# The v tile asked for behind the store and the x tile: SyncE's order of requests in the mixing stage of a two-layer kernel on one Trainium2 core

## The chip, the cores and the metric

The kernel runs on one core of one Trainium2 chip. The metric is the device time of one execution in microseconds (us), as the median over several runs. Lower is better. The core has five engines with a queue of instructions each: PE (TensorE, matmuls), DVE (VectorE), ACT (ScalarE), POOL (GpSimd) and SP (SyncE, which computes nothing and here only waits and issues DMA transfers). DMA transfers that SP issues appear in the profile as hardware queue q1, those that POOL issues as software queue q0.

## What is computed

The input x is (2, 48, 512, 512) in float32. Layer 0 adds to x a channel attention over 4x4 blocks, and layer 1 adds to that four directional scans. Cut to what the change touches:

```
# layer 0, on the normalized x
qkv = depthwise3x3(conv1x1(x))               # q, k, v, in 8 heads
q, k, v -> (b, heads, 6 * 4 * 4 = 96, 128 * 128)
attn = softmax(q_hat @ k_hat.T * temperature)     # 96 x 96 for each head
out = attn @ v                               # MIXING: this stage
out = proj 1x1 (48 channels) of out, put back in rows and columns
x1 = x + out                                 # MIXING: the sum with x
# layer 1: x1 + four scans (down, up, right, left) of the normalized x1
```

## The kernel before, in words

The program has five stages, one after the other: statistics of x, a first pass over x that makes q, k and v and writes v to DRAM (`v_blocks`), the mixing, the four scans, and a final sum. The change touches the mixing stage alone, in `attention_weights_and_mix`.

Mixing first computes the 96x96 attention weights (`attT`). Then it goes over 64 groups: 2 batches (`B`) of 32 groups (`G`), and a group is 16 image rows of 48 channels (`T` = 16). A group is 4 tiles of 4 rows (`NB` = 4). For group j the engines do this:

- PE: for each of the 4 tiles, 8 matmuls per head set with the v tile (`a_ps<-attT,v_in`, L812; the function `group`), whose end counts up the semaphore `att_done`; 8 transposes (`t_ps<-eye,mixed`, L800; `turn`); and two projections (`o_ps<-turned,projd`, L790; `project`). The projections in group j are those of group j - 1: PE works one group behind itself there.
- ACT copies between PSUM and SBUF for PE (L848, L853).
- DVE: four times per group it adds the projected rows in PSUM to the rows of x (`scan_t<-o_ps,res`, L931, four instructions), which counts up the semaphore `summed`, and takes statistics (`bn_stats`, L942, two instructions). It does this for group j - 1 while PE mixes group j.
- SP: three transfers for each group: the next v tile (`load_v`, L698, 1536 KB on 96 partitions, into one of two slots of `v_in`), the store of the lower half of the finished sum (`store`, L691, `x_scan<-scan_t`, 768 KB on 48 partitions), and the lower half of the x tile (`load_res`, L685, `res<-x`, 768 KB on 48 partitions).
- POOL: two transfers for each group, the upper halves of that store and of that x tile (`upper_half`, the same two lines).

What orders SP's requests is the order in which they are written, and two waits. A v slot is free when PE has mixed the group that used it, so the load of v(j + 1) waits for `att_done` of 4j (all tiles of group j - 1 mixed). The store of group j - 2 waits until `summed` shows that group as added up; the x tile of group j then goes into the slot that those sums have left. SP waits in order: what stands behind a waiting instruction is not issued. The waits of the engines that use the data are these: PE waits at the start of group j + 1 for its v tile (`v_landed`), and DVE waits before its first sum of group j for both halves of the x tile and for the stores that free the slot of `scan_t` (`res_landed`, `scan_out`).

The rounds of the loop `Fori(1, G // 2 - 1)` do this for most groups, and `turnover` for the four groups at a batch's two ends. The first three v tiles are asked for ahead of all this and do not move.

Of the kernel before, what the change touches and what calls it, by code (L numbers as in the profile page):

```python
# [638 lines left out]
def attention_weights_and_mix(nc, sem, sumsq, ones, gram_sb, temp, eye, x, projT, attT, v_blocks, x1_scan, x1_stats, x1_mv):  # L639
# [5 lines left out]
    with ExitStack() as ctx:  # L645
# [35 lines left out]
        def batch_of(j):  # L681
            return divmod(j, G)

        def load_res(queue, b, g, s, half):
            queue.dma_start(res[ODD * half:ODD * half + C, s],  # L685
                            x[b, :, bass.ds(T * g + NP * half, NP)]).then_inc(res_landed[half][s], 16)

        def store(queue, b, g, s, q):

            queue.wait_ge(summed, N * G * b + N * g + N)  # L690
            queue.dma_start(x1_scan[b, :, bass.ds(g, 1), q].rearrange("c g t w -> c (g t) w"),  # L691
                            scan_t[ODD * q:ODD * q + C, s]).then_inc(scan_out[q][s], 16)

        with nc.Block() as block:
            @block.sync
            def _(sp):
                def load_v(b, g, s):
                    sp.dma_start(v_in[:, s].rearrange("p h i n -> p h (i n)"),  # L698
                                 v_blocks[b, bass.ds(g, 1)].rearrange("g p h n -> (g p) h n")).then_inc(v_landed[s], 16)

                def next_v(j):

                    sp.wait_ge(att_done, NB * j)
                    load_v(*batch_of(j + 1), (j + 1) % 2)

                def turnover(j):

                    if j + 1 < GROUPS:
                        next_v(j)
                    store(sp, *batch_of(j - 2), j % 2, 0)  # L710
                    load_res(sp, *batch_of(j), j % 2, 0)

                sp.dma_start(temp_sb[:], temp.broadcast_to([HD, HEADS])).then_inc(params, 16)
                for s in range(2):
                    load_v(0, s, s)
                sp.wait_ge(proj_clear, 1)
                for q in range(2):
                    sp.dma_start(projd[ODD * q:ODD * q + C, ODD * q:ODD * q + C], projT).then_inc(proj_in, 16)
                for s in range(2):
                    load_res(sp, 0, s, s, 0)  # L720
                next_v(1)
                for b in range(B):
                    if b:
                        turnover(b * G)
                        turnover(b * G + 1)
                    with sp.Fori(1, G // 2 - 1) as i:
                        for s in range(2):

                            sp.wait_ge(att_done, NB * G * b + NB * (2 * i + s))
                            load_v(b, 2 * i + s + 1, 1 - s)  # L730
                            store(sp, b, 2 * i + s - 2, s, 0)
                            load_res(sp, b, 2 * i + s, s, 0)
                    turnover(b * G + G - 2)
                    turnover(b * G + G - 1)
                for s in range(2):
                    store(sp, B - 1, G - 2 + s, s, 0)
                for s in range(2):
                    sp.wait_ge(scan_out[0][s], 16 * (GROUPS // 2))
# [783 lines left out]
```

## Time and profile before

| what | value |
|---|---|
| median of 3 runs | 10613.97 us (10603.93 to 10615.23) |
| the profiled execution, its own time | 10620.18 us |
| its span, first to last instruction | 10618.6 us |
| PE busy over the span | 9390.0 us (88%) |
| DVE busy over the span | 8088.3 us (76%) |
| DMA traffic | 2101.31 MB, mean 198 GB/s |

The rows further down come from the profiled execution, so a sum worked out from them is made against its 10620.18 us, and that is 6.2 us above the median. PE's busy time is modelled at its ends, so a busy PE is not a PE at its peak; idle gaps on PE are real waits.

### The profile page before, as it was taken

The numbers are of one execution on the slowest core, as the hardware profiler recorded it, in microseconds if no ns is written. First come the engines' busy times: TensorE is split into PE (matmuls) and PEld (weight loads), VectorE is DVE, ScalarE is ACT, GpSimd is POOL, SyncE is SP. The second block draws the span as 40 slices with busy tenths as digits, with TensorE's granted clock in tenths as the row PEclk, the third lists the DMA queues.
The fourth block names the chain that finished last, engine by engine and source line by source line (L and its number), as shares of the span: only waits on it lengthen the run. The fifth ranks groups of instructions, "written<-read, shape, count | busy, mean of one in ns | idle before, by whom it ended". The sixth has DMA issues, their size and how long they took to land. (4 is left out here: it accounts for less than half of the span.)

```text
span 10618.6 us, 213374 instructions
## 1 busy us (share of the span) xinstructions
PE 9390.0 (88%) x72742; PEld 9046.5 (85%) x72742; DVE 8088.3 (76%) x16184; ACT 6343.3 (60%) x11046; POOL 2941.8 (28%) x4237
## 2 busy tenths in 40 slices
PE   0799999999999998999979999999999999999200
PEld 0699999999999998777769999999999999999200
DVE  7777777777777776888877777777799997777333
ACT  0577777767777776443446667999933336666100
POOL 0000000000000000000026666666666666666100
PEclk9999999999999999999989999999999999999655
DMA  9566666666666666899978897777766666777899
GB/s 365 121 131 132 132 131 129 132 118 133 133 132 130 132 133 118 238 256 247 261 174 202 201 202 183 210 214 214 211 208 217 214 212 171 205 199 198 338 431 406
DMA packets 726580, 2101.31 MB, mean 198 GB/s; under 512 B 56944, under 2 KB 631568, under 8 KB 635360
## 3 DMA queue, kind: packets, MB, share of 16 engines
q1 hardware_dynamic: 611920, 1794.63, 65.9%
q10 hardware_dynamic: 106368, 204.76, 6.2%
q0 software_dynamic: 8192, 100.67, 3.4%
q8 instruction: 51, 0.84, 0.0%
q14 instruction: 49, 0.40, 0.0%
HBM read 1344.64 MB, written 754.97 MB: 198 GB/s over the span
## 5 line engine op out<-in xcount | busy, mean ns | idle before, releaser
L1363 ACT CAST hi<-rough 112x256 fp32r<-112x256 f32 x4096 | 1666.9, 407 | 1402.5 <-DVE rough L1277 1352.7
L1197 PE MATMUL scan_ps<-hi,scan_high 112*112 112x256 f32 x12264 | 2123.3, 281 | 32.3 <-ACT hi L1363 32.3
L1277 DVE SCALAR_TENSOR_TENSOR rough<-scan_ps,scan_bias,lines 112x256 f32<-112x256 f32 x4086 | 2136.7, 523 | 18.7 <-issue 15.0
L1208 PE MATMUL scan_ps_low<-lo,scan_high 112*112 112x256 f32 x12264 | 2126.3, 282 | 0.5 <-POOL lo L1309 0.5
L1203 PE MATMUL scan_ps_low<-hi,scan_low 112*112 112x256 f32 x12264 | 2121.4, 281 | 0.0
L488 PE MATMUL conv_ps<-tap_high,x_high 128*128 128x432 f32 (+2 forms) x6144 | 1879.3, 306 | 45.1 <-DVE x_edge L568 31.7
L488 PE MATMUL conv_ps<-tap_low,x_high 128*128 128x432 f32 (+2 forms) x6144 | 1906.6, 310 | 0.0
L488 PE MATMUL conv_ps<-tap_high,x_low 128*128 128x432 f32 (+2 forms) x6144 | 1906.4, 310 | 0.0
L1197 PEld LDWEIGHTS scan_ps<-hi,scan_high 112*112 112x112 f32 x12264 | 1691.2, 176 | 33.7 <-ACT hi L1363 33.1
L1208 PEld LDWEIGHTS scan_ps_low<-lo,scan_high 112*112 112x112 f32 x12264 | 1686.3, 175 | 3.4 <-POOL lo L1309 0.9
L1203 PEld LDWEIGHTS scan_ps_low<-hi,scan_low 112*112 112x112 f32 x12264 | 1684.0, 176 | 0.0
L1309 POOL TENSOR_TENSOR lo<-lines,hi 112x256 fp32r<-112x256 f32 x2048 | 1418.5, 693 | 802.7 <-DVE lines L1282 779.4
L1309 POOL TENSOR_TENSOR lo<-ring,hi 112x256 fp32r<-112x256 f32 x2048 | 1419.8, 693 | 769.1 <-DVE ring L1282 763.8
L368 ACT ACTIVATE x_high<-raw,negmean 128x512 fp32r<-128x512 f32 x1024 | 1217.2, 1247 | 62.5 <-DMA raw_edge<-x 51.5
L564 DVE SCALAR_TENSOR_TENSOR x_low<-raw,negmean,x_high 128x512 fp32r<-128x512 f32 x1024 | 1150.3, 1153 | 118.9 <-ACT x_high L368 118.9
L1282 DVE TENSOR_TENSOR ring<-scan_ps_low,rough 112x256 f32<-112x256 f32 x2044 | 869.0, 425 | 467.9 <-PE scan_ps_low L1208 432.3
L488 PEld LDWEIGHTS conv_ps<-tap_high,x_high 128*128 128x128 f32 x6144 | 1161.5, 189 | 66.6 <-DVE x_edge L568 33.3
L488 PEld LDWEIGHTS conv_ps<-tap_low,x_high 128*128 128x128 f32 x6144 | 1162.5, 189 | 20.8 <-issue 0.2
L488 PEld LDWEIGHTS conv_ps<-tap_high,x_low 128*128 128x128 f32 x6144 | 1165.0, 190 | 17.3
L1282 DVE TENSOR_TENSOR lines<-scan_ps_low,rough 112x256 f32<-112x256 f32 x2044 | 868.7, 425 | 302.2 <-PE scan_ps_low L1208 220.8
L742 POOL MEMSET projd<- 112x112 f32 x1 | 0.2, 192 | 3882.8 <-POOLq L322 3882.8
L405 ACT COPY qk<-conv_ps 128x288 f32<-128x288 f32 x1024 | 415.1, 405 | 959.2 <-PE conv_ps L494 957.9
(138 smaller groups left out, 12741.3 us busy)
## 6 DMA issues: line engine op xcount, KB each, us to landing
raw<-x SPq DMA_DIRECT2D x764, 256.0 KB, 5.4
d_rows<-lines SPq DMA_DIRECT2D x32, 3584.0 KB, 30.5
u_cols<-lines SPq DMA_DIRECT2D x64, 1792.0 KB, 13.4
r_cols<-lines SPq DMA_DIRECT2D x32, 3584.0 KB, 24.4
lines<-u_cols SPq DMA_DIRECT2D x31, 3584.0 KB, 16.6
lines<-r_cols SPq DMA_DIRECT2D x30, 3584.0 KB, 16.5
lines<-d_rows SPq DMA_DIRECT2D x30, 3360.0 KB, 15.6
xs<-x SPq DMA_DIRECT2D x24, 4096.0 KB, 12.5
```

The costliest lines, as they stand in the source:

```text
L368: ins = nc.scalar.activation(x_high[:, s, k, :, 1:TOK + 1], phases(raw, s, k), ACT.Identity, bias=negmean0[:, 0, b:b + 1], scale=1.0)
L405: nc.scalar.copy(qk_at(i % 2, dy, 0, 3), qk_of(left))
L488: nc.tensor.matmul(bank(dy, side, lo - side, hi - side), xs[at], ws[taps], start=fresh[side], stop=False, skip_group_check=True)
L564: ins = nc.vector.scalar_tensor_tensor(x_low[:, s, k, :, 1:TOK + 1], phases(raw, s, k), negmean0[:, 0, b:b + 1], x_high[:, s, k, :, 1:TOK ...
L742: nc.gpsimd.memset(projd[:], 0.0).then_inc(proj_clear, 1)
L1197: last = nc.tensor.matmul(ps[:, b, 0:LP], high[:, shift], hi[:, b, (k - 1) % 2, shift:shift + LP], start=shift == 0, stop=shift == 2)
L1203: nc.tensor.matmul(ps_low[:, b, 0:LP], low[:, shift], hi[:, b, (k - 1) % 2, shift:shift + LP], start=shift == 0, stop=False)
L1208: last = nc.tensor.matmul(ps_low[:, b, 0:LP], high[:, shift], lo[:, b, shift:shift + LP], start=False, stop=shift == 2)
L1277: nc.vector.scalar_tensor_tensor(rough[:, b, k % 2], ps[:, b, 0:LP], bias, line(way, s, k % T, b, kept), ALU.add, ALU.add).then_inc(rough_ ...
L1282: nc.vector.tensor_tensor(state(way, s, k, b), ps_low[:, b, 0:LP], rough[:, b, k % 2], ALU.add).then_inc(state_done[b], 1)
L1309: nc.gpsimd.tensor_tensor(lo[:, b, 1:LP + 1], state(way, k // T, k, b), hi[:, b, k % 2, 1:LP + 1], ALU.subtract).then_inc(lo_ready[b], 1)
L1363: nc.scalar.copy(hi[:, b, k % 2, 1:LP + 1], rough[:, b, k % 2]).then_inc(hi_ready[b], 1)
```

## The change

In the two places where SP's three requests for a group are written, the wait for `att_done` and the v load move behind the store and the x tile. Nothing is added or removed, and no other engine's list changes (the line numbers behind the place go down by one).

```diff
                 def turnover(j):
 
+                    store(sp, *batch_of(j - 2), j % 2, 0)
+                    load_res(sp, *batch_of(j), j % 2, 0)
                     if j + 1 < GROUPS:
                         next_v(j)
-                    store(sp, *batch_of(j - 2), j % 2, 0)
-                    load_res(sp, *batch_of(j), j % 2, 0)
...
                     with sp.Fori(1, G // 2 - 1) as i:
                         for s in range(2):
-
+                            store(sp, b, 2 * i + s - 2, s, 0)
+                            load_res(sp, b, 2 * i + s, s, 0)
                             sp.wait_ge(att_done, NB * G * b + NB * (2 * i + s))
                             load_v(b, 2 * i + s + 1, 1 - s)
-                            store(sp, b, 2 * i + s - 2, s, 0)
-                            load_res(sp, b, 2 * i + s, s, 0)
```

SP's queue before, from the request ahead of the loop through one group of the loop (`v_in<-v_blocks` is the v load, `x_scan<-scan_t` the store, `res<-x` the x tile; ISA and REGISTER_ALU rows compute addresses or wait; the semaphore that a row waits for is in brackets):

```order
L698 DMA v_in<-v_blocks 96x4096 [waits att_done]
L726 UNCONDITIONAL_BRANCH
L726 ISA
L698 ISA [waits att_done]
L698 DMA v_in<-v_blocks 96x4096
L690 ISA
L691 ISA [waits summed]
L691 DMA x_scan<-scan_t 48x4096
L685 ISA
L685 DMA res<-x 48x4096
```

In each group the v load waits for `att_done` alone, and the wait for `summed` stands behind it.

SP's queue after the change, the same place:

```order
L698 DMA v_in<-v_blocks 96x4096 [waits att_done]
L726 UNCONDITIONAL_BRANCH
L726 ISA
L691 ISA [waits summed]
L691 DMA x_scan<-scan_t 48x4096
L685 ISA
L685 DMA res<-x 48x4096
L730 REGISTER_ALU
L698 ISA [waits att_done]
L698 DMA v_in<-v_blocks 96x4096
```

The v load has moved behind the wait for `summed` and behind two transfers of the same queue.

## Rows read from the trace of the kernel before

**Rows 1.** Windows: us, busy us of the engines, granted clock, DMA share, GB/s.

```profile
4247.00:5440.00 1193.00, 1146.73 (x7168) 874.80 (x7168) 1046.39 (x1539) 481.31 (x768) 65.50 (x126) 0.97 0.94 248
5000.00:5100.00 100.00, 100.00 (x644) 76.63 (x643) 89.83 (x134) 43.07 (x70) 6.24 (x12) 1.00 0.99 270
```

**Rows 2.** Waits from 4280 to 5420 us: total us, times, longest us.

```profile
DVE scan_t L931 <- DMA res<-x: 50.3, 20, 5.5
...
PE o_ps L790 <- DVE scan_t L931: 28.0, 12, 5.6
```

**Rows 3.** PE's timeline: start, us, line, operation, what ended an idle time.

```profile
5288.14 1.92 PE L812 MATMUL a_ps<-attT,v_in 96*128 96x96 f32 x16
...
5292.49 1.04 PE L800 MATMUL t_ps<-eye,mixed 128*112 128x128 f32 x8
5293.37 1.92 PE L812 MATMUL a_ps<-attT,v_in 96*128 96x96 f32 x16
...
5310.79 1.92 PE L812 MATMUL a_ps<-attT,v_in 96*128 96x96 f32 x16
```

**Rows 4.** SP's timeline: start of each request, us to issue it.

```profile
5223.44 0.34 SPq L691 DMA_DIRECT2D x_scan<-scan_t  x1
5223.98 0.32 SPq L685 DMA_DIRECT2D res<-x  x1
5231.86 0.32 SPq L698 DMA_DIRECT2D v_in<-v_blocks  x1
...
5290.25 0.32 SPq L698 DMA_DIRECT2D v_in<-v_blocks  x1
5295.67 0.34 SPq L691 DMA_DIRECT2D x_scan<-scan_t  x1
5296.21 0.32 SPq L685 DMA_DIRECT2D res<-x  x1
5307.68 0.32 SPq L698 DMA_DIRECT2D v_in<-v_blocks  x1
```

**Rows 5.** The tile v_in from 4280 to 5420 us: its loads on SP.

```profile
L698 SPq DMA_DIRECT2D v_in<-v_blocks x61: 312/317/327, 4281.6 to 5377.2; - x61
```

**Rows 6.** DVE's timeline around the sums of one group's last and the next's first rows.

```profile
5292.69 2.80 DVE L931 TENSOR_TENSOR scan_t<-o_ps,res 48x512 f32<-48x512 f32 x4
...
5314.49 2.79 DVE L931 TENSOR_TENSOR scan_t<-o_ps,res 48x512 f32<-48x512 f32 x4
```

**Rows 7.** DMA issues from 5290 to 5297 us: KB, us from issue to landing.

```profile
v_in<-v_blocks SPq DMA_DIRECT2D x1, 1536.0 KB, 11.0
x_scan<-scan_t SPq DMA_DIRECT2D x1, 768.0 KB, 10.4
...
res<-x SPq DMA_DIRECT2D x1, 768.0 KB, 17.2
res<-x POOLq DMA_DIRECT2D x1, 768.0 KB, 16.9
```

**Rows 8.** DMA issues from 5307 to 5308 us: KB, us from issue to landing.

```profile
v_in<-v_blocks SPq DMA_DIRECT2D x1, 1536.0 KB, 10.9
```

**Rows 9.** DMA issues from 5223 to 5232 us: KB, us from issue to landing.

```profile
v_in<-v_blocks SPq DMA_DIRECT2D x1, 1536.0 KB, 14.4
x_scan<-scan_t SPq DMA_DIRECT2D x1, 768.0 KB, 6.7
...
res<-x SPq DMA_DIRECT2D x1, 768.0 KB, 11.8
res<-x POOLq DMA_DIRECT2D x1, 768.0 KB, 20.5
```

**Rows 10.** PE's timeline at two of its seven gaps above 2 us.

```profile
4861.41 3.75 PE L790 MATMUL o_ps<-turned,projd 112*112 112x512 f32 x4 [5.59 <-DVE scan_t L931]
...
5248.17 2.77 PE L790 MATMUL o_ps<-turned,projd 112*112 112x512 f32 x4 [2.55 <-DVE scan_t L931]
```

**Rows 11.** Windows of 2 us behind the longest gap: columns as in rows 1.

```profile
4858.00:4860.00 2.00, 0.00 (x0) 0.00 (x0) 1.96 (x4) 0.00 (x0) 0.00 (x0) 1.00 1.04 328
4860.00:4862.00 2.00, 0.59 (x1) 0.45 (x2) 1.95 (x4) 0.00 (x0) 0.00 (x0) 0.52 0.71 180
...
4868.00:4870.00 2.00, 2.00 (x11) 2.00 (x11) 1.94 (x4) 0.88 (x2) 0.00 (x0) 0.50 0.43 90
4870.00:4872.00 2.00, 2.00 (x7) 0.93 (x6) 0.93 (x2) 1.01 (x1) 0.00 (x0) 0.92 0.97 262
```

## The prediction

> **What bounds the kernel now.** I first cut the trace into its stages, to see what the engines do where the change is. The mixing stage is 1193 us of the span, with PE busy for 1146.73 us of it, the granted clock at 0.97 and the DMA engines busy for 0.94 of the time [rows 1]. In a stretch without trouble all three are full: PE 100.00 of 100 us, DMA share 0.99 at 270 GB/s, DVE 89.83 [rows 1]. So in this stage PE and the DMA engines are both near their limit, and what counts is not how much is moved but what lands when.
>
> Next, PE's own rhythm. The first mixing matmuls of one group start at 5293.37 and those of the next at 5310.79 [rows 3]: a group takes 17.42 us when nobody waits. The waits show what disturbs that: DVE waited 50.3 us in 20 pieces for the x tile (res), up to 5.5 us, and PE in turn 28.0 us in 12 pieces for DVE's sums [rows 2]. No row has PE waiting for a v tile. What the disturbance costs is in the v requests, one per group: 61 of them lie between 4281.6 and 5377.2 [rows 5], 60 intervals in 1095.6 us, where 60 x 17.42 would be 1045.2. The loss is 50.4 us. This is all that a better order of SP's requests could win here.
>
> Then the queue itself. Call I the moment at which SP issues a group's store. In the undisturbed group I is 5295.67 and the v request for the next group stands at 5290.25, 5.42 us ahead of it [rows 4], just behind the end of the mixing matmuls that free its slot (5288.14 + 1.92 = 5290.06 [rows 3]). That v tile lands 11.0 us later, at 5301.25 [rows 7], and PE needs it at 5310.79: 9.5 us to spare. The x tile of SP, issued at 5296.21, lands 17.2 us later at 5313.4 [rows 4, 7], and POOL's half lands about then; DVE first uses it at 5314.49 [rows 6], so about 1 us to spare. The scarce slack is on the x tile, and the v tile has plenty. That is what speaks for the change, and the question is whether 9.5 us is enough for what the v tile loses.
>
> **The change, part by part.** Nothing is computed anew; on SP 61 v loads (v(3) to v(63), rows 5) go behind the store and the x tile of their group. The store's wait ends with DVE's sums (5292.69 + 2.80 = 5295.49 [rows 6]), as before, so I does not move by itself. The v request is issued right behind the x tile, at about I + 1.0 (0.54 from store to x tile in rows 4, and about as much again), 6.4 us later than now. Taken alone these 6.4 us fit into the 9.5.
>
> But the v tile is then also behind 1536 KB in SP's own queue, and this is the expensive part. When does it land? The trace holds the answer, since in disturbed groups SP got to the v request while its earlier transfers still ran. At I = 5223.44 the store landed after 6.7 us, the x tile at 5223.98 + 11.8 = 5235.8 (I + 12.3), POOL's x tile, asked for about 1 us behind I, 20.5 us after that, and the next v tile, asked for at 5231.86 and so already queued when SP's x tile landed, at 5231.86 + 14.4 = 5246.26: I + 22.8 [rows 4, 9]. That is the order of the changed kernel. In the undisturbed group the next v tile, asked for 12.0 us behind I (5307.68), landed at 5318.6: I + 22.9 [rows 4, 8]. So two request times, 3.6 us apart against I, gave the same landing: the transfers in front decide it, not the request. I take 22.8.
>
> PE needs that v tile at the start of the next group. I lies 2.30 us behind a group's start S (5293.37 to 5295.67 [rows 3, 4]), and the next start is S + 17.42, so the need is at I + 15.1. The tile is 22.8 - 15.1 = **7.7 us late**.
>
> A stall also moves the next deadline. The store of a group waits for sums that PE has already fed before it stalls, so I stays 2.30 us behind the moment at which PE *could* have started, while the following group ends later by the stall w. So the next tile is late by 7.7 - w. A stall of 7.7 us is followed by none, and that by 7.7 again; or both are 3.85. Either way it is 7.7 us for two groups: 61 loads make 31 long waits (v(3), v(5), ..., v(63)), 31 x 7.7 = 238.7 us.
>
> A price on top is the clock. After PE's gaps above 2 us the granted clock fell: behind the gap of 5.59 us the windows show 0.52 and 0.50, one of the two levels (1.2 GHz instead of 2.4), from about 4860 until 4870, and there the four projections took 3.75 us [rows 10, 11]. PE's waits make up 28.0 of the 50.4 us lost; the other 22.4 us fell behind seven gaps of 2.2 to 5.59 us (two of them in rows 10), 3.2 us for each. The bounds for the gap of 7.7 us are 0 and, by the longest gap, about half of 8.6 us (4861.4 to 4870), 4.3 us. I take 3.2, the mean: the clock will fall partly while PE idles anyway. 31 x 3.2 = 99.2 us. As the clock's loss falls into the long pair's slack, it delays the next group and takes nothing from the next wait, which is zero already.
>
> What is won: the x tile of SP now has only the store in front of it and lands at I + 12.3 (against 17.7 in rows 4 and 7), POOL's at about I + 21.6 at worst (rows 9), and DVE needs it no sooner than it does now, 5314.49 - 5295.67 = I + 18.8, plus the 7.7 us by which PE is late. The waits for res go, and with them the 50.4 us.
>
> Sum: 10620.2 + 238.7 + 99.2 - 50.4 = 10907.7 us by the profiled execution, which stood 6.2 us above the median, so 10901.5; I say **10900 us**.
>
> Here a rule and the rows differ. SP's store of 768 KB took 6.7 us with nothing ahead of it [rows 9], and all five transfers of a group (4.72 MB) took 22.8 us from I. The Trainium skill (DMA: Bandwidth & Descriptors, Anatomy of one DMA) gives a transfer about 2.0 us plus its bytes at 436 GB/s. By that, as an estimate, the store would take 3.8 us, and the five together some 12.8 us; the v tile would be in time and the sum would be 10620.2 - 50.4 = 10569.8. The measured rows decide against it, and I keep 22.8.
>
> **The rivals.**
>
> *Hidden, and so faster.* If the v tile landed before I + 15.1, PE would never wait for it and only the gain is left: 10620.2 - 50.4 - 6.2, about 10564 us. The five transfers would have to need 15.1 us, a third less than in both groups that I read. For it: the DMA share of 0.94 to 0.99 counts stretched transfers, and another order could pack better: the v tile needed only 5.2 us behind the x tile (I + 17.7 to I + 22.9, rows 4, 7 and 8), a rate of 300 GB/s where the stage has 248 [rows 1]. Against it: in the undisturbed group the DMA engines are busy 0.99 of 17.42 us [rows 1], so five transfers in 15.1 us were never seen. The Trainium skill's formula above is the rule that would bring this. Chance 0.05.
>
> *Late, but the clock hardly falls.* If the wait settles at 3.85 us per group or the clock falls inside the wait only, 99.2 us shrink to between 0 and 40: 10802 to 10842 us. For it: a short gap cost little. Against it: each gap above 2 us in the trace had a fall behind it. Chance 0.23.
>
> *Late and worse.* A landing at I + 23.5 and the clock price of the longest gap: 31 x (8.4 + 4.3) = 393.7 us, less 50.4: 10957 us; with a slow clock for a whole group more, up to 11000. Chance 0.17.
>
> *Late, but better packed.* With v running beside POOL's x tile the v tile lands at I + 18: 31 x 2.9 = 90 us, less 50.4, near 10653 us. For it: that rate of 300 GB/s of v alone. Against it: rows 9 had that very overlap. Chance 0.08; a quarter of this comes out within 0.2% or under.
>
> *The likeliest*, 10850 to 10950 us, has 0.47.
>
> **How the numbers follow.** 0.2% is 21 us, about what a measurement of this kernel tells from no change. Faster: 0.05 plus a little of the better packed case, 0.06. The same: 0.02. Slower: 0.92. The range leaves out the two cheap cases (0.13) and the far end of the costly one: 10790 (no clock price, 10802, and a little less) to 10985.
>
> **What the changed profile would show.** The v request about 1.0 us behind the store, and the v landing about 22 us behind it (not 15). A new row in the waits, PE's mixing matmuls or their weights waiting for DMA v_in, 31 or more times and 200 to 260 us in total. The row for res gone or near zero. The granted clock in the mixing stage well under 0.97, about 0.85 to 0.9. The stage longer by some 290 us and every other stage as it was. If PE's waits for v are short of 100 us, the landing time is the step that failed; if they are as said and the time is under 10850, the clock's price is.

## The result, and the profile after

The changed kernel takes 10991.24 us (median; 10984.93 to 11010.78) against 10608.95 us of the kernel before in the same measurement: a ratio of 1.0365, 95% interval 1.0347 to 1.0383. It is slower, as forecast, but by 382 us where 286 us over the runs then known were forecast, and just outside the range (up to 10985). The profiled execution has a span of 10983.4 us, 364.8 us more than before, and the sums further down explain these 364.8 us. The other 17.5 us of the 382 come from which execution was profiled: before, it stood 11.2 us above the median of this measurement, and after, 6.3 us below.

The stages come first. Windows of the changed kernel, with columns as in rows 1:

```profile
0.00:4247.00 4247.00, 3860.66 (x28770) 3794.04 (x28770) 3213.34 (x6341) 2879.19 (x4132) 24.11 (x13) 0.99 0.68 144
4247.00:5800.00 1553.00, 1240.86 (x7176) 938.33 (x7176) 1050.41 (x1541) 481.69 (x770) 65.28 (x126) 0.85 0.76 191
```

By these windows the mixing stage is 360 us longer than the 1193 us of [rows 1]; from the first mixing matmul to the last it is 354 us longer (4251.0 to 5769.7 us, before 4247.1 to 5411.8). DVE has the same busy time in it (1050 against 1046 us), while PE's has grown by 94 us, which are the same matmuls at a lower clock (0.85 against 0.97), and the DMA share has fallen from 0.94 to 0.76: the DMA engines, nearly full before, now stand idle for a quarter of the stage.

The waits of the same stage (4280 to 5780 us) answer to [rows 2]:

```profile
DVE scan_t L930 <- PE o_ps L789: 408.1, 66, 14.6
...
PE a_ps L811 <- DMA v_in<-v_blocks: 288.6, 31, 10.6
```

PE waits 31 times for a v tile, 9.31 us each. The waits for res are gone from the list. PE's timeline at one of the 31, with SP's queue in the same groups:

```profile
4881.28 1.04 PE L799 MATMUL t_ps<-eye,mixed 128*112 128x128 f32 x8
4891.08 3.72 PE L811 MATMUL a_ps<-attT,v_in 96*128 96x96 f32 x16 [8.77 <-DMA v_in<-v_blocks]
4894.60 3.65 PE L789 MATMUL o_ps<-turned,projd 112*112 112x512 f32 x4
...
4902.79 1.92 PE L811 MATMUL a_ps<-attT,v_in 96*128 96x96 f32 x16
```

```profile
4867.02 0.34 SPq L691 DMA_DIRECT2D x_scan<-scan_t  x1
4867.55 0.32 SPq L685 DMA_DIRECT2D res<-x  x1
4868.13 3.11 SPq L698 DMA_DIRECT2D v_in<-v_blocks  x1
4884.45 0.34 SPq L691 DMA_DIRECT2D x_scan<-scan_t  x1
...
4914.66 0.34 SPq L691 DMA_DIRECT2D x_scan<-scan_t  x1
```

The v request stands 1.1 us behind the store (4867.02). Stores are 17.43 and then 30.21 us apart: a group with no wait, then one with a long wait in it. The rhythm of two holds through the stage: the first and the last of the 31 waits end at 4317.21 and 5752.80 us, 30 pairs of groups in 1435.6 us, 47.85 us for a pair where two undisturbed groups take 34.84. The DMA issues from 4867 to 4870 us, with KB and us to landing, answer to [rows 9]:

```profile
v_in<-v_blocks SPq DMA_DIRECT2D x1, 1536.0 KB, 22.8
x_scan<-scan_t SPq DMA_DIRECT2D x1, 768.0 KB, 6.7
x_scan<-scan_t POOLq DMA_DIRECT2D x1, 768.0 KB, 17.1
res<-x SPq DMA_DIRECT2D x1, 768.0 KB, 12.6
res<-x POOLq DMA_DIRECT2D x1, 768.0 KB, 23.0
```

The v tile lands at 4868.13 + 22.8 = 4890.9, 23.9 us behind the store, and PE starts 0.2 us later. In the prediction's words, with I for the moment of a group's store, that is I + 23.9. POOL's x tile takes 23.0 us, where it took 20.5 in [rows 9]. The group is no exception. All 61 v loads of the stage, and below them those of the kernel before, took from request to landing:

```profile
DMA to landing us min/median/max: 19.4/22.6/24.2
```

```profile
DMA to landing us min/median/max: 9.0/12.2/16.5
```

The granted clock in windows of 2 us around that wait (rows as in rows 11):

```profile
4884.00:4886.00 2.00, 0.00 (x0) 0.00 (x0) 1.56 (x3) 0.00 (x0) 0.96 (x2) 0.80 0.92 156
4886.00:4888.00 2.00, 0.00 (x0) 0.00 (x0) 0.00 (x0) 0.00 (x0) 0.08 (x1) 0.50 1.06 295
...
4896.00:4898.00 2.00, 2.00 (x3) 0.65 (x2) 0.00 (x0) 0.00 (x0) 0.00 (x0) 0.50 1.13 229
4898.00:4900.00 2.00, 2.00 (x16) 1.96 (x15) 1.69 (x3) 0.00 (x0) 0.00 (x0) 0.79 0.99 172
```

The clock falls some 3 us into the wait, and about 8 us at the lower level (1.2 GHz) lie behind its end: the mixing matmuls of one tile take 3.72 us instead of 1.92, the projections 3.65 instead of 1.88.

### The profile page after: what moved, and what is told of

The parts are those of the page before. It is cut to its first block and busy times, and to the rows that moved or that the text cites. A ratio compares the mean times of both kernels' runs of the same rounds, so it can differ in the third digit from the quotient of the medians.

```text
span 10983.4 us, 213374 instructions
## 1 busy us (share of the span) xinstructions
PE 9488.1 (86%) x72742; PEld 9114.3 (83%) x72742; DVE 8083.8 (74%) x16184; ACT 6341.0 (58%) x11046; POOL 2937.6 (27%) x4237
## 5 line engine op out<-in xcount | busy, mean ns | idle before, releaser
L930 DVE TENSOR_TENSOR scan_t<-o_ps,res 48x512 f32<-48x512 f32 x1024 | 705.2, 689 | 465.1 <-PE o_ps L789 432.5
## 6 DMA issues: line engine op xcount, KB each, us to landing
r_cols<-lines SPq DMA_DIRECT2D x32, 3584.0 KB, 24.4
lines<-u_cols SPq DMA_DIRECT2D x31, 3584.0 KB, 16.6
lines<-r_cols SPq DMA_DIRECT2D x30, 3584.0 KB, 16.4
```

The lines of the kernel that those rows point to most:

```text
L930: ins = nc.vector.tensor_tensor(scan_t[ODD * q:ODD * q + C, s, at:at + N + 1:N].rearrange("p i (j two) -> p i j two", two=2), o_ps[ODD * q ...
```

## The experiments

All ran on one core as the kernel does. In the order of their runs: the moved wait, the store first, the busy PE and the late request shared one chip and its runs of the kernel before (10625.9 us); the change once more, the small x tile, the third v slot and v on ACT another set (10628.14 us); the third x slot ran by itself (10624.69 us).

**The change once more**, as the reference of the second set.

> The changed kernel once more, beside the next three on the same chip, as their reference: 10990 us, 3.65% over the kernel before, with 31 long waits of 9.3 us for the v tile.

10992.81 us, ratio 1.0349 (1.0332 to 1.0366). Its profile has the same 31 waits for v, 292.9 us.

**Only the wait moved.** The transfers stay in the order of before.

```diff
-                            sp.wait_ge(att_done, NB * G * b + NB * (2 * i + s))
+                            sp.wait_ge(summed, N * G * b + N * (2 * i + s - 2) + N)
                             load_v(b, 2 * i + s + 1, 1 - s)
                             store(sp, b, 2 * i + s - 2, s, 0)
                             load_res(sp, b, 2 * i + s, s, 0)
```

(The sums of a group come behind the mixing for which `att_done` was waited for, so the second wait covers the first.)

> The order of before (v, store, x tile), but SP waits for the sums of group j - 2 ahead of all three, so the v request moves 5.4 us later (it is issued about when the store is) and nothing is put in front of it in the queue. If the bytes in front of v set its landing (my account), v lands some 6 to 8 us behind the request, PE never waits for it, and the time stays within 0.5% of before: 10600 to 10660 us, the store and the x tile landing about 1 us later and the waits for the x tile somewhat longer. If it is the lateness of the request (the rival), PE waits for v in this kernel too and the time comes near that of the change, 10900 to 11000 us.

10710.29 us, ratio 1.0079 (1.0062 to 1.0096). The profile has no wait of PE for v: asked for 5.4 us later than in the kernel before, v lands 12.2 us behind its request in the group that I read (issued at 4970.35; the median of the 61 loads is 10.5), well ahead of its need, if not after the 6 to 8 us that I expected. So the lateness of the request is not what costs the 382 us. It is not free either. The waits for the x tile have grown from 50.3 us to (stage of this kernel, 4280 to 5560 us):

```profile
DVE scan_t L931 <- DMA res<-x: 140.0, 58, 5.3
```

My expectation of at most 10660 us was too low by 50: I had the right row and too small a number.

**The store first, then v, then the x tile.**

```diff
                             store(sp, b, 2 * i + s - 2, s, 0)
-                            load_res(sp, b, 2 * i + s, s, 0)
                             sp.wait_ge(att_done, NB * G * b + NB * (2 * i + s))
                             load_v(b, 2 * i + s + 1, 1 - s)
+                            load_res(sp, b, 2 * i + s, s, 0)
```

> The order store, v, x tile: half the bytes of the change stand in front of v. My account: the store lands at I + 6.7 and v at I + 12 to 14, ahead of its need at I + 15.1, so PE does not wait for v; but SP's x tile is last and lands at I + 17.5 to 20, where DVE needs it at I + 18.8: waits for the x tile of 0 to 3 us in many groups, 10600 to 10750 us. The rival, that any place behind the store is too late: waits for v of 200 us or more and 10850 us or more.

10848.36 us, ratio 1.0208 (1.0191 to 1.0225). Between the two accounts, and my landing time was wrong. The waits of the stage:

```profile
PE a_ps L811 <- DMA v_in<-v_blocks: 140.2, 41, 8.0
...
DVE scan_t L930 <- DMA res<-x: 52.9, 13, 4.7
```

In the group whose store was issued at 5048.59 (v at 5049.22) v took 15.9 us and landed at I + 16.5, where I had expected I + 12 to 14: POOL's store of 768 KB, landing after 16.4 us, was moved beside it. With 768 KB less in front of it in SP's queue than in the change, v landed 7.4 us sooner behind the store in the groups that I read (I + 16.5 against I + 23.9).

**PE kept busy through the wait.** The changed kernel, with 84 (`KEEP_BUSY`) transposes whose results nobody reads, in the odd groups:

```diff
+                    if s == 1 and not second:
+                        for _ in range(KEEP_BUSY):
+                            nc.tensor.transpose(a_ps[:, 0, 4 * HD:512], eye[:], eye[:])
                     pe.wait_ge(v_landed[s], 8 * (j - s) + 16)
```

> The changed kernel with 84 small transposes (128x128, results unused) that PE runs ahead of its wait for the v tile in the odd groups, where all 31 long waits fall; at 0.109 us each they fill the 9.3 us for which PE sat idle. If the granted clock falls because PE idles, it now stays at its upper level and each pair of groups takes 2 x 17.42 + 9.2 = 44.0 us instead of 47.9: 31 x 3.7 = 115 us less than the changed kernel, about 10875 us. If the slower matmuls behind the wait have another cause, such as the load's own traffic, the time stays at 10990 us.

10901.02 us, ratio 1.0258 (1.0241 to 1.0276); against the change's 10991.24 and 10992.81 that is 90 to 92 us less, where 115 were expected. A window of the stage (4300 to 5400 us) and PE behind one of its waits:

```profile
4300.00:5400.00 1100.00, 1086.63 (x7554) 882.82 (x7554) 799.81 (x1179) 367.99 (x587) 51.98 (x100) 1.00 0.85 211
```

```profile
5090.99 2.02 PE L816 MATMUL a_ps<-attT,v_in 96*128 96x96 f32 x16 [0.83 <-DMA v_in<-v_blocks]
5092.85 1.90 PE L789 MATMUL o_ps<-turned,projd 112*112 112x512 f32 x4
```

The clock is at 1.00 and the matmuls behind the wait are back at 2.02 and 1.90 us. From the first tile behind the transposes (4323.94) to the last (5670.49) the 30 pairs of groups take 44.89 us each, against 47.85 in the changed kernel, and 31 x 2.96 = 92 us is the measured gain. Beyond two undisturbed groups (34.84 us) a pair still holds 10.0 us, the 9.2 to 9.3 us of transposes and a rest in which PE waits 16.1 us for v in all. The expected pair was 44.0 us, and this is where the missing 24 us are. That the clock falls because PE idles is shown, and about 91 us of the change's loss are due to it.

**v asked for when SP's x tile has landed.**

```diff
                             load_res(sp, b, 2 * i + s, s, 0)
-                            sp.wait_ge(att_done, NB * G * b + NB * (2 * i + s))
+                            sp.wait_ge(res_landed[0][s], 8 * (G * b + 2 * i) + 16)
                             load_v(b, 2 * i + s + 1, 1 - s)
```

> The changed order, but SP asks for v only once its x tile has landed, some 11 us later still. If the landing is set by the bytes in front, v lands about 1.5 us later than in the changed kernel, for the latency that is no longer hidden: I + 26, 31 x 1.5 = 45 us more, 11030 us. If an early place in the queue makes the transfers in flight slower (the changed kernel's v landed at I + 24.5 where in the kernel before it landed at I + 22.8), v lands at I + 22 to 23 and the time falls to about 10940 us.

10996.41 us, ratio 1.0340 (1.0321 to 1.0358): no difference from the change. So neither 45 us more nor 50 less. In the queue, though, something did happen. The issues of the group whose store is at 4868.86 us (v asked for at 4881.58):

```profile
v_in<-v_blocks SPq DMA_DIRECT2D x1, 1536.0 KB, 10.7
...
x_scan<-scan_t POOLq DMA_DIRECT2D x1, 768.0 KB, 13.4
res<-x SPq DMA_DIRECT2D x1, 768.0 KB, 12.0
res<-x POOLq DMA_DIRECT2D x1, 768.0 KB, 16.6
```

v landed at I + 23.4. It was asked for 11.6 us later than in the changed kernel's group above and landed 0.5 us *earlier* behind its store. POOL's store and x tile took 13.4 and 16.6 us against 17.1 and 23.0. So a v request that stands in the queue early slows POOL's transfers while they run, and gains nothing for v. PE's waits for v are 267.6 us against 288.6, and the time does not show it. The trace says where the gain went. The first wait is 21.85 us instead of 10.63: v was held back until 4304.89 us by an x tile that took 17.7 us, and then took 18.6 itself. The other 30 have shrunk from 9.26 to 8.19 us, but a pair of groups takes 47.55 us (4323.64 to 5750.08) against 47.85: what it holds beyond two undisturbed groups and the wait has grown from 3.7 to 4.5 us. In the group above the lower level of the clock lasts some 8.5 us behind the wait (to about 4900.8), where it was 7.8:

```profile
4900.00:4902.00 2.00, 2.00 (x16) 2.00 (x16) 1.96 (x4) 0.00 (x1) 0.00 (x0) 0.79 0.43 107
```

The 30 pairs together are 9 us shorter, the first wait 11 us longer.

**POOL's x tile cut to one row of eight** (this leaves out seven eighths of the upper half of x in the sum, from the third group on).

```diff
+            rows = 1 if half and not whole_tile else NP
-            queue.dma_start(res[ODD * half:ODD * half + C, s],
-                            x[b, :, bass.ds(T * g + NP * half, NP)]).then_inc(res_landed[half][s], 16)
+            queue.dma_start(res[ODD * half:ODD * half + C, s, 0:rows],
+                            x[b, :, bass.ds(T * g + NP * half, rows)]).then_inc(res_landed[half][s], 16)
```

> The changed kernel with POOL's x tile cut to one row of eight after the first two groups (the output is then not the reference's). It takes 672 KB a group off the other queue and leaves SP's queue as it is. If the two queues share the DMA engines, v lands 3 to 5 us sooner behind the store (I + 20 instead of I + 24.5), the long waits shrink from 9.3 to about 5 us and the time falls by 120 to 180 us, to about 10830 us. If v waits only for what stands ahead of it in its own queue, v lands at I + 24 as before and the time stays within 20 us of 10990.

10888.25 us, ratio 1.0249 (1.0232 to 1.0267): 105 us less than the change. The issues at a store at 5000.68 us (v asked for at 5001.85), and the waits:

```profile
v_in<-v_blocks SPq DMA_DIRECT2D x1, 1536.0 KB, 19.7
```

```profile
PE a_ps L812 <- DMA v_in<-v_blocks: 149.3, 31, 6.8
```

v lands at I + 20.9 and the wait is 4.8 us instead of 9.31. v's landing depends on the other queue too: without 672 KB of POOL's it came 3.0 us sooner in the groups that I read, less than the 7.4 us for 768 KB in front of it in SP's own queue (the store first, above). The time fell by less than the 120 us expected, and less than 31 x 4.5 = 140 us. The clock accounts for the difference. From 4311.46 to 5641.97 us the 30 pairs of groups take 44.35 us each, 4.8 us beyond two undisturbed groups and the wait, where the changed kernel's have 3.7: 31 x 1.1 = 34 us, which leaves 106.

**A third v slot.** The order of the change, with v asked for one group earlier. `third` is the memory of the sums of squares and of the gram matrix, which nobody reads once the attention weights are made. SP's and PE's loops over the groups are written out.

```diff
                 sp.wait_ge(att_done, NB * j)
-                load_v(*batch_of(j + 1), (j + 1) % 2)
+                load_v(*batch_of(j + 2), (j + 2) % 3)
...
+        v_slots = (v_two[:, 0], v_two[:, 1], third)
```

> The changed order (store, x tile, v), but with a third v slot, laid over memory that is free in this stage, so that SP asks for the v tile of group j + 2 where it asked for that of j + 1, and v is needed 17.4 us later. If the change costs its time because v misses its deadline, PE no longer waits for v, the queue runs v, store, x tile in a circle as it does in the kernel before, and the time is that of before within 0.4%: 10570 to 10650 us. If this order needs more than 17.4 us of DMA time for a group, the queue itself sets the pace and the time is 10700 us or more with waits for the x tile or v in nearly all groups.

10762.78 us, ratio 1.0130 (1.0113 to 1.0147). PE no longer waits for v, and 230 us of the 365 by which the change is slower in this set are gone: that much hung on v's deadline. But the x tile is now late (waits, 4280 to 5560 us, and DVE at one of them):

```profile
DVE scan_t L917 <- DMA res<-x: 179.6, 30, 8.1
```

```profile
4970.96 2.79 DVE L917 TENSOR_TENSOR scan_t<-o_ps,res 48x512 f32<-48x512 f32 x4 [5.81 <-DMA res<-x]
```

It is POOL's half: asked for at 4947.71 it took 23.0 us. In the changed kernel it is as late, but PE is later still, for v, so no wait shows. The expectation named waits for the x tile and 10700 us or more as the sign that the queue itself sets the pace. The time agrees with it, but the waits come in every other group (30), not in nearly all.

**v asked for by ACT**, in a hardware queue of its own, behind the copy of a group's last tile:

```diff
                         take(1, i % 2).then_inc(taken, 1)
+                        if i == NB - 1 and not last:
+                            act.dma_start(v_in[:, s].rearrange("p h i n -> p h (i n)"),
+                                          v_all[bass.ds(j + 2, 1)].rearrange("g p h n -> (g p) h n")).then_inc(v_landed[s], 16)
```

> The v load leaves SP and is issued by ACT, behind its copy of a group's last tile, so at the moment at which the kernel before asks for it but in a hardware queue of its own. SP keeps store and x tile. If what counts is only that v was in SP's queue, this is the best of both and PE and DVE wait for nothing: 10560 to 10590 us. If the queues share the engines, v now takes its part from the x tiles that are still in flight when it is asked for, these land 1 to 3 us later, and DVE waits for them in most groups: 10620 to 10750 us.

10716.33 us, ratio 1.0090 (1.0074 to 1.0107). The waits for the x tile are 148.9 us in 30 pieces, 3 times those of before. A queue of its own did not bring v in sooner either: from request to landing its loads took 14.4 us (median), against 12.2 in the kernel before.

**A third slot for the x tile**, in the order of before. This was to be the version that beats both.

```diff
-                    load_res(sp, *batch_of(j), j % 2, 0)
+                    if j + 1 < GROUPS:
+                        load_res(sp, *batch_of(j + 1), (j + 1) % 3, 0)
```

(The same on POOL; DVE reads slot j % 3; the loops of the three are written out.)

> The order of the kernel before (v, store, x tile), but with a third slot for the x tile, laid over memory that is free in this stage, and each x tile asked for one group earlier by SP and by POOL. The transfers and their order in the queues stay, only the x tile's deadline moves 17.4 us back. If the kernel before loses its 50 us to the deadline of the x tile alone, the waits for res go, the clock stays up and the time is 10560 to 10580 us, 0.4 to 0.5% faster. If the DMA engines cannot move five transfers in 17.42 us for long, the loss comes back as waits for v or for the stores, and the time is 10600 us or more.

10619.23 us, ratio 0.9997 (0.9985 to 1.0010), with runs from 10585.53 to 10649.24: no gain is shown, and the interval allows at most 16 us. The waits for res are gone, and two others have come (4280 to 5440 us):

```profile
DVE scan_t L915 <- DMA x_scan<-scan_t: 11.3, 10, 1.8
PE a_ps L796 <- DMA v_in<-v_blocks: 9.0, 7, 2.4
```

Why is seen in two v loads, one issued at 4308.59 and one at 4796.54 us:

```profile
v_in<-v_blocks SPq DMA_DIRECT2D x1, 1536.0 KB, 12.2
```

```profile
v_in<-v_blocks SPq DMA_DIRECT2D x1, 1536.0 KB, 22.6
```

In 28 groups without a stall the landing of v has slipped by 10.4 us, 0.37 us a group: the DMA engines need about 17.8 us for five transfers and the compute engines 17.42. In that stretch they are never idle:

```profile
4300.00:4800.00 500.00, 499.98 (x3211) 383.14 (x3209) 463.05 (x689) 216.05 (x345) 28.72 (x56) 1.00 1.00 267
```

The 61 v loads lie between 4291.2 and 5362.0 us, 17.85 us apart, 25.6 us in all above 60 x 17.42. In the kernel before that loss was 50.4 us. So, by these two profiled executions, about half of it is left, and it fits the DMA engines' own pace (60 x 0.37 = 22 us); the other half went with the x tile's earlier request. The profiled execution's mixing did end earlier (ACT's first work for the scans stands at 5454.90 instead of 5470.56 us), but its span is only 4.4 us shorter. In the timed runs no gain stands out from the spread; where the other 11 us went is not shown.

## Why the prediction was wrong in size

**The deadline and the rhythm: right.** v is needed 15.1 us behind the store, it lands behind the 1536 KB in front of it, PE waits in every other group and not between: 31 waits, as counted. The third v slot shows that the waits hang on this deadline.

**The landing at I + 22.8: mis-sized, and this is the step that failed.** It is the largest part of the miss. The tile was to be 7.7 us late and was 9.31. In the group above it landed at I + 23.9; a wait of 9.31 stands for I + 24.4. I had read 22.8 from two groups in which v was asked for 8.4 and 12.0 us behind the store, and said that the request time did not matter since both gave the same. It does, from the other side: asked for at I + 1.1, v runs beside POOL's store and x tile from the start of its turn, and all of them finish later (17.1 and 23.0 us for POOL's two, against 13.4 and 16.6 when v is asked for behind the x tile). So the step "the transfers in front decide it, not the request" was wrong. The experiment with the late request shows it for POOL's transfers, and for v by the waits (8.19 us against 9.26): 1.1 of the 1.6 us. The other 0.5 us and the way in which the DMA engines share are not shown. 31 x 1.6 = 50 us.

**The clock at 3.2 us for each wait: a little low.** 47.85 - 34.84 - 9.31 = 3.7 us. 31 x 0.5 = 16 us. The term was a mean over seven shorter gaps, 2.2 to 5.6 us, and nothing tied it to a wait of 9 us. That it came so close is partly luck: where the wait was 4.75 us the clock took 4.8. That PE's idling is its cause, which the prediction only had from rows side by side, the run with the busy PE shows.

**The gain of 50.4 us: it fits the sum, for a reason that was too simple.** The waits for res did go, though no run measures the 50.4 us by itself. I wrote, however, that the x tile would land at I + 12.3 and, from POOL, at I + 21.6 at worst and so be in time. POOL's lands at about I + 24 and would be late, as the kernel with three v slots shows. It is in time only because PE is later.

**The sum.** 31 x (9.31 + 3.70) - 50.4 = 352.9 us, against 287.5 in the prediction and 364.8 in the spans. Of the other 12 us, 4 lie ahead of the first mixing matmul (4251.0 against 4247.1 us), 1 in the stage, and 7 behind it (ACT's first work for the scans starts at 5828.54 instead of 5470.56 us, 358.0 later); I don't explain them. The median was missed by 91 us: 66 by the two terms, these 12, and the rest because the changed kernel's profiled execution stood 6.3 us below its median, where I had taken it to stand 6.2 us above, and by rounding. PE's waits for v, 288.6 us, lie outside the 200 to 260 that I wanted to see in the profile; the granted clock, 0.85, is as said.

**The range.** The costly rival had this case in it (31 x (8.4 + 4.3)), at 10957 us and up to 11000, and got 0.17. The range cut its far end off.

**The 436 GB/s formula** of the Trainium skill (DMA: Bandwidth & Descriptors, Anatomy of one DMA) gave as an estimate 12.8 us for a group's five transfers; measured are 17.8 us when the queues are never empty, and 24 from an idle start. The section fits it to transfers that GpSimd issues, and I used it for SP's too. SP's store of 768 KB on 48 partitions, the first in idle queues, took 6.7 us, where the formula's estimate is 3.8; it was not alone, the x tile behind it was moving too. The Trainium skill (SBUF — State Buffer, Door 1) makes the bandwidth depend on how many of the 16 ports a transfer's partitions reach. The trace agrees in direction. While only SP's two halves moved, both on the lower 48 partitions, the DMA engines showed a share of 0.97 and 184 GB/s, where a full stretch has 0.99 and 270 [rows 1]:

```profile
4868.00:4872.00 4.00, 4.00 (x28) 3.16 (x27) 3.67 (x7) 1.76 (x3) 0.56 (x2) 1.00 0.97 184
```

No run here changed the number of partitions, so that this is the reason is not shown.

## What to carry to other kernels

A transfer that has slack in a trace has it at its present place in the queue: before moving it back, add up what is then in front of it and what the other queues have in flight at that time, and set that against its deadline. In a stage with the DMA engines as full as here (share 0.94), a wait for one tile can be the place where their shortage shows: a later request and another queue for v made the waits for the x tile longer, a third v slot moved the change's waits from v to the x tile, and a third x slot took the waits away but only about half of the stage's loss. And a wait of PE that comes back in a rhythm costs more than its length, since the clock falls with it: here 3.7 us on top of 9.3, and 4.8 us on top of waits half as long. To shorten such a wait gives back less than its length; only the run that left PE no gap got the clock's part back.

## What the runs showed of the hardware

- A transfer asked for 11.6 us earlier landed later behind its store (I + 23.9 against I + 23.4), and beside it two transfers of another queue took 3.7 and 6.4 us longer.
- SP's request for v took 3.11 us in the group above (median 2.66 of 61), 1.1 us behind the store and 0.6 behind the x tile; in the kernel before it takes 0.32 us. Three requests of the same sizes within 1.4 us are not enough for it: with only the wait moved, in the order v, store, x tile, each took 0.32 to 0.34 us. What holds SP is not shown.
- The wait's price in clock grew as the wait shrank: 3.7 us on 9.3, 4.5 us on 8.2, 4.8 us on 4.75.
- The granted clock stayed up with PE filled by transposes whose results nobody reads (1.00 over 1100 us), and fell in the 31 long waits without them: behind each the mixing matmuls ran at the lower level (3.72 or 3.73 us for a tile instead of 1.92).
